# Maxima rows on ScalarE's DMA queue, normalised rows written by ScalarE, and a respaced step table in a fused attention and FFN kernel

## The reference, cut to what matters

```
x = x + L0_xattn(ln(x), ctx)     # 16 heads of 16; queries and keys normalised per head; softmax over 1601 keys
x = x + L0_ffn(ln(x))            # 256 -> 64 -> 1024, gelu, -> 64 -> 256
x = x + L1_xattn(ln(x), ctx)     # one head of 16, scores normalised per query row; the output tiled 16 times
x = x + L1_ffn(ln(x))            # soft mixture over 2048 slots; its softmax runs over the 16 batches
ln(x) = (x - mean) / sqrt(var + 1e-5)
```

## Time and profile before

| | |
|---|---|
| median of 3 runs | 6414.54 us (6410.36 to 6420.31) |
| the profiled execution | 6438.05 us, span 6436.0 us |
| TensorE matmuls busy | 5770.0 us, 90% of the span |
| TensorE weight loads busy | 2996.8 us, 47% |
| VectorE busy | 3625.0 us, 56% |
| ScalarE busy | 3263.2 us, 51% |
| GpSimd busy | 2413.9 us, 38% |
| granted TensorE clock, mean | 0.955 |
| score matmuls of stage one | from 245.1 to 4394.6 us |

### The profile page before, as it was taken

The page is one execution under the profiler, slowest core; times in us unless marked ns, Lnnn a source line. Parts: engine busy times, 40 slices in busy tenths (PEclk is TensorE's granted clock), DMA queues, the critical chain, the costliest instruction groups (busy, mean ns, idle before and its releaser), DMA issues. The chain is left out here.

```text
span 6436.0 us, 94456 instructions
## 1 busy us (share of the span) xinstructions
PE 5770.0 (90%) x36221; PEld 2996.8 (47%) x36221; DVE 3625.0 (56%) x7015; ACT 3263.2 (51%) x6257; POOL 2413.9 (38%) x2686
## 2 busy tenths in 40 slices
PE   3799999999999998999989999896599999998999
PEld 1223333333333332333323333232488888877888
DVE  3565656656666665665666656660466666652333
ACT  1366666666665666666666666663222222223331
POOL 3226356263462644626436355344122222220000
PEclk9799999999999999999999999997799999999999
DMA  2441432414324233242332432310366666666553
GB/s 57 86 86 50 78 70 63 85 51 77 70 68 83 54 77 66 70 82 60 68 67 71 79 68 65 64 23 16 135 220 214 213 215 210 208 219 243 205 196 118
DMA packets 436274, 683.75 MB, mean 106 GB/s; under 512 B 63376, under 2 KB 336928, under 8 KB 433520
## 3 DMA queue, kind: packets, MB, share of 16 engines
q1 hardware_dynamic: 326000, 568.64, 34.4%
q10 hardware_dynamic: 109824, 109.07, 5.0%
HBM read 458.39 MB, written 218.39 MB: 105 GB/s over the span
## 5 line engine op out<-in xcount | busy, mean ns | idle before, releaser
L1271 DVE TENSOR_REDUCE mx<-psum 128x1 f32<-128x401 f32 x4096 | 2166.8, 569 | 1570.2 <-PE psum L810 1565.1
L1107 ACT ACTIVATE probs<-psum 128x512 f32<-128x512 f32 (+1 forms) x3328 | 1894.1, 601 | 907.9 <-PE psum L832 900.9
L810 PE MATMUL psum<-kst,qst 96*128 96x401 bf16 x4096 | 1365.1, 348 | 86.0 <-DMA qst<-q_planes 35.9
L832 PE MATMUL psum<-qst,kst 99*128 99x512 bf16 (+1 forms) x3328 | 1302.1, 392 | 109.7 <-ACT probs L1107 58.7
L810 PEld LDWEIGHTS psum<-kst,qst 96*128 96x128 bf16 x4096 | 406.3, 99 | 1339.5 <-DVE mx L1271 900.5
L843 PE MATMUL psum<-probs,vaug 128*17 128x512 f32 x6656 | 903.0, 615 | 0.0
L1565 POOL TENSOR_TENSOR disp<-disp,rz 128x2048 f32<-128x2048 f32 x64 | 294.4, 4601 | 930.3 <-DVE rz L1795 930.3
L832 PEld LDWEIGHTS psum<-qst,kst 99*128 99x128 bf16 (+1 forms) x3328 | 335.0, 101 | 522.7 <-ACT probs L1107 262.9
L1584 PE MATMUL psum<-phi,xT 128*128 128x128 f32 x4096 | 514.3, 280 | 39.6 <-DMA xT<-xnT_scratch 33.6
L1599 PE MATMUL psum<-disp,xnb 128*128 128x128 f32 x4096 | 492.7, 279 | 52.9 <-DMA xnb<-xn_scratch 34.2
L1584 PEld LDWEIGHTS psum<-phi,xT 128*128 128x128 f32 x4096 | 482.6, 194 | 87.3 <-issue 80.9
(11 more groups left out here) (198 smaller groups left out, 7467.5 us busy)
## 6 DMA issues: line engine op xcount, KB each, us to landing
xnb<-xn_scratch SPq DMA_DIRECT2D x256, 512.0 KB, 3.7
kst<-k_planes SPq DMA_DIRECT2D x384, 200.1 KB, 8.8
logit_scratch<-disp ACTq DMA_DIRECT2D x64, 1024.0 KB, 4.9
xT<-logit_scratch SPq DMA_DIRECT2D x32, 2048.0 KB, 7.9
k_planes<-pl SPq DMA_DIRECT2D x96, 384.0 KB, 3.2
y_scratch<-ysb ACTq DMA_DIRECT2D x128, 256.0 KB, 4.9
vaug<-v_scratch SPq DMA_DIRECT2D x64, 442.0 KB, 3.7
v_scratch<-vst SPq DMA_DIRECT2D x48, 544.0 KB, 3.1
```

Source lines behind the costliest of these rows:

```text
L810: mm(to[:, 0:PW], qst[g][0:NP, j, t * P:(t + 1) * P], kst[g][0:NP, j, k0:k0 + PW], start=True, stop=True).then_inc(m_full, 1)
L832: mm(bank[S_BANK[n % 2]][0:m, :], kst[g][0:NR, j, c * P:c * P + m], qst[g][0:NR, j, :], start=True, stop=True).then_inc(s_full, 1)
L1107: fn(probs[0:m, 4 * (k % 2) + j, :], bank[S_BANK[j % 2]][0:m, :], ACT.Exp, scale=float(HD) ** 0.5).then_inc(s_exp, 1)
L1271: v.tensor_reduce(mx[:, n % 2, u // 4, u % 4:u % 4 + 1], bank[HOMES[r][0]][:, 0:PW], AX.X, ALU.max).then_inc(m_free, 1)
```

## The change

The three maxima transfers are issued by ScalarE, one after each of its first three exponentials of step 12 of a group. `lna` on GpSimd keeps only the root and makes a shift (minus mean times root) in two more small operations, and signals `ln_root`. A new item `lnx` on ScalarE writes the four tiles as `Identity` with that scale and bias. `V1` 4 to 7 get entries in `HEAD_BANK`, whose pace goes from 0.82 to 0.72. Most positions of the tail move. Bank 7 is lent out one step longer.

```diff
-    + [("kv1", 1), ("X", 1, 0), ("X", 1, 1), ("T", 3, 0), ("T", 3, 1), ("K", 8), ("K", 9), ("X", 2, 0), ("K", 10),
-       ("X", 2, 1), ("K", 11), ("kv1", 2), ("T", 4, 0), ("K", 12), ("kv1", 3), ("X", 3, 0), ("X", 3, 1), ("X", 4, 0)])
-HEAD_PACE = 0.82
+    + [("kv1", 1), ("X", 1, 0), ("X", 1, 1), ("V1", 4), ("T", 3, 0), ("V1", 5), ("T", 3, 1), ("V1", 6), ("K", 8),
+       ("V1", 7), ("K", 9), ("X", 2, 0), ("K", 10), ("X", 2, 1), ("K", 11), ("kv1", 2), ("T", 4, 0), ("K", 12), ("kv1", 3),
+       ("X", 3, 0), ("X", 3, 1), ("X", 4, 0)])
+HEAD_PACE = 0.72
...
-        put(head[done] + 0.7, 1, "ssq", n)
-        put(head[done] + 0.72, 1, "kn", n)
+        put(head[done] + 1.0, 1, "ssq", n)
+        put(head[done] + 1.02, 1, "kn", n)
...
-    put(5.67, -1, "proj", 1)
-    put(6.34, -1, "res", 1, 1)
+    put(6.0, -1, "proj", 1)
+    put(6.67, -1, "res", 1, 1)
     for t in range(QT):
-        put((5.67, 6.0, 6.67, 7.0)[t], -1, "bns", 1, t)
-        put((26.0, 26.35, 26.67, 27.0)[t], -1, "bns", 2, t)
-        put((45.67, 46.0, 46.67, 47.0)[t], -1, "bns", 3, t)
-    put(7.34, -1, "lnv", 1)
-    put(7.35, -1, "lna", 1)
-    put(7.36, -1, "base", 2)
+        put((5.67, 6.0, 7.0, 7.34)[t], -1, "bns", 1, t)
+        put((26.67, 27.0, 27.34, 27.67)[t], -1, "bns", 2, t)
+        put((45.67, 46.34, 47.0, 47.34)[t], -1, "bns", 3, t)
+    put(7.67, -1, "lnv", 1)
+    put(7.68, -1, "lna", 1)
+    put(8.34, -1, "lnx", 1)
+    put(8.35, -1, "base", 2)
...
-        put((11.34, 12.0, 12.67, 13.34, 16.67, 17.67, 18.36, 20.0)[f], -1, "V1", f)
-        put((11.67, 12.34, 13.0, 13.67, 17.0, 18.0, 19.0, 20.34)[f], -1, "gpre", f)
-        put((12.67, 13.34, 14.0, 14.67, 18.34, 19.34, 20.34, 21.34)[f], -1, "gtanh", f)
-        put((12.68, 13.35, 14.01, 14.68, 18.35, 19.35, 20.35, 21.35)[f], -1, "gpost", f)
+        if f < 4:
+            put((11.0, 11.67, 12.34, 13.0)[f], -1, "V1", f)
+        put((11.34, 12.0, 12.67, 13.34, 16.34, 17.67, 19.0, 20.67)[f], -1, "gpre", f)
+        put((12.34, 13.0, 13.67, 14.34, 17.34, 18.67, 20.0, 21.67)[f], -1, "gtanh", f)
+        put((12.35, 13.01, 13.68, 14.35, 17.35, 18.68, 20.01, 21.68)[f], -1, "gpost", f)
     for p in range(FC // 2):
-        put((16.34, 18.34, 21.67, 23.67)[p], -1, "U2", p)
+        put((15.34, 17.0, 21.0, 23.67)[p], -1, "U2", p)
...
-    put(25.34, -1, "res", 2, 0)
-    put(25.67, -1, "v2", 1)
-    put(26.34, -1, "res", 2, 1)
-    put(27.34, -1, "lnv", 2)
-    put(27.35, -1, "lna", 2)
-    put(27.36, -1, "base", 3)
-    put(29.0, -1, "xT", 2, 0)
+    put(25.67, -1, "res", 2, 0)
+    put(26.0, -1, "v2", 1)
+    put(26.67, -1, "res", 2, 1)
+    put(28.0, -1, "lnv", 2)
+    put(28.01, -1, "lna", 2)
+    put(28.67, -1, "lnx", 2)
+    put(28.68, -1, "base", 3)
+    put(29.67, -1, "xT", 2, 0)
...
-        put((36.0, 37.0, 38.34, 39.34, 40.67, 41.67, 43.0)[p], -1, "s1", p)
+        put((36.34, 37.34, 38.67, 39.67, 41.0, 42.0, 43.0)[p], -1, "s1", p)
...
-        put((44.67, 45.0, 45.67, 46.0)[t], -1, "out", t)
-        put((45.34, 45.67, 46.34, 46.67)[t], -1, "res", 3, t)
-    put(47.34, -1, "lnv", 3)
-    put(47.35, -1, "lna", 3)
+        put((44.67, 45.0, 46.0, 46.34)[t], -1, "out", t)
+        put((45.34, 46.0, 46.67, 47.0)[t], -1, "res", 3, t)
+    put(47.67, -1, "lnv", 3)
+    put(47.68, -1, "lna", 3)
+    put(48.34, -1, "lnx", 3)
...
-LENT = [s < 38 or s > 46 for s in range(STEPS)]
+LENT = [s < 38 or s > 47 for s in range(STEPS)]
...
-            def normalised(b, k):
+            def root_and_shift(b, k):
                 pool.wait_ge(ln_var, at("ln_var", b, "lnv", k))
...
                 link(pool.tensor_tensor(rs[:, :], rs[:, :], powers[:, 0:1].broadcast_to((P, QT)), ALU.pow))
-                for t in range(QT):
-                    ins = pool.tensor_scalar(xn[:, t, :], xw[:, t, :], mv[:, t, 0:1], rs[:, t:t + 1],
-                                             ALU.subtract, ALU.mult)
-                ins.then_inc(xn_ready, 1)
+                link(pool.tensor_tensor(nb[:, :], mv[:, :, 0], rs[:, :], ALU.mult))
+                pool.tensor_scalar(nb[:, :], nb[:, :], -1.0, None, ALU.mult).then_inc(ln_root, 1)
...
+            def load_maxima(n, r):
+                if r == 0:
+                    act.wait_ge(nm_ready, n + 1)
+                act.dma_start(qst[n % G][96 + r:97 + r, :, :].rearrange("o j (t q) -> o (j t) q", q=P),
+                              nT[:, r, :]).then_inc(nm_loaded, 16)
...
+            def normalised(b, k):
+                act.wait_ge(ln_root, at("ln_root", b, "lna", k))
...
+                for t in range(QT):
+                    ins = fn(xn[:, t, :], xw[:, t, :], ACT.Identity, bias=nb[:, t:t + 1], scale=rs[:, t:t + 1])
+                ins.then_inc(xn_ready, 1)
...
+                    def maximum_row(r):
+                        if c == MAX_STEP + 1 and n + 1 < B * G:
+                            load_maxima(n + 1, r)
+
                     exponentials(b, g, c, 0)
+                    maximum_row(0)
...
                     exponentials(b, g, c, 1)
+                    maximum_row(1)
...
                     exponentials(b, g, c, 2)
+                    maximum_row(2)
```

More of the change, by code:

```diff
@@ L72, in woven @@
     for label, pos in head.items():
-        put(pos, 1, *label)
+        put(pos, -1 if label[0] == "V1" else 1, *label)
     put(2.0, 1, "ln0v")
@@ L141, in woven @@
     put(1.0, -1, "kc")
-    put(31.0, -1, "cq")
-    put(31.67, -1, "cqe")
-    put(32.34, -1, "cs")
+    put(31.67, -1, "cq")
+    put(32.0, -1, "cqe")
+    put(32.67, -1, "cs")
     put(33.0, -1, "cse")
@@ L180 @@
     "pv1": ("t_mm",), "o1": ("t_act",), "out": ("t_mm",), "res": ("t_dve",), "bns": ("ln_sum",), "lnv": ("ln_var",),
-    "lna": ("xn_ready",), "base": ("based",)}
+    "lna": ("ln_root",), "lnx": ("xn_ready",), "base": ("based",)}
 def plane_buffer(b, at, label):
@@ L274, in ring_uses @@
         if home == 7:
-            b = (k - 47) // STEPS
-            if last[7] is not None and k >= 47 and (back[7] - 47) // STEPS < b:
+            b = (k - 48) // STEPS
+            if last[7] is not None and k >= 48 and (back[7] - 48) // STEPS < b:
                 homes[i] = (home, last[home], b - 1)
@@ L388, in stage_one @@
         rs = sb("rs", [P, QT])
+        nb = sb("nb", [P, QT])
         pT = sb("pT", [P, S])
@@ L444, in stage_one @@
         ln_var = sem("ln_var")
+        ln_root = sem("ln_root")
         xn_ready = sem("xn_ready")
@@ L587, in store_tail @@
                 sp.dma_start(xnT_d[b], xnT[:, :, :]).then_inc(x_stored, 16)
[L589 to L593, removed]
             steps = {"ld": load_block, "stV": store_values, "stkv1": store_keys_one, "stX": store_planes,
@@ L601, in _ @@
             alone(-1, steps)
-            load_maxima(0)
             for b in range(B):
                 for s in range(STEPS):
-                    n, c = b * G + s // KC, s % KC
-                    if c == MAX_STEP + 1 and n + 1 < B * G:
-                        load_maxima(n + 1)
                     for place in range(3):
@@ L669, in base @@
                 else:
-                    pool.wait_ge(xn_ready, at("xn_ready", b, "lna", k - 1))
+                    pool.wait_ge(xn_ready, at("xn_ready", b, "lnx", k - 1))
                 bias = (bpr, b2r, bor)[k - 1]
@@ L673, in base @@
                                    ALU.add).then_inc(based, 1)
-            def normalised(b, k):
+            def root_and_shift(b, k):
                 pool.wait_ge(ln_var, at("ln_var", b, "lnv", k))
-                if k == 1 and b >= 1:
-                    pool.wait_ge(x_stored, at("x_stored", b - 1, "st3"))
+                before = at("ln_root", b, "lna", k) - 1
+                if before >= 1:
+                    pool.wait_ge(xn_ready, before)
                 link(pool.tensor_scalar(rs[:, :], mv[:, :, 1], EPS, None, ALU.add))
                 link(pool.tensor_tensor(rs[:, :], rs[:, :], powers[:, 0:1].broadcast_to((P, QT)), ALU.pow))
-                for t in range(QT):
-                    ins = pool.tensor_scalar(xn[:, t, :], xw[:, t, :], mv[:, t, 0:1], rs[:, t:t + 1],
-                                             ALU.subtract, ALU.mult)
-                ins.then_inc(xn_ready, 1)
+                link(pool.tensor_tensor(nb[:, :], mv[:, :, 0], rs[:, :], ALU.mult))
+                pool.tensor_scalar(nb[:, :], nb[:, :], -1.0, None, ALU.mult).then_inc(ln_root, 1)
             def gelu_inside(b, f):
@@ L714, in score_inverse @@
                 pool.tensor_tensor(sg[:, :], sg[:, :], powers[:, 2:3].broadcast_to((P, QT)), ALU.pow).then_inc(sc_inv, 1)
-            steps = {"ln0a": first_norm, "kn": scaled, "X": planes, "base": base, "lna": normalised,
+            steps = {"ln0a": first_norm, "kn": scaled, "X": planes, "base": base, "lna": root_and_shift,
                      "gpre": gelu_inside, "gpost": gelu_outside, "kc": keys_centred, "sgp": score_inverse}
@@ L870, in transpose_x @@
                 if h == 0:
-                    pe.wait_ge(xn_ready, at("xn_ready", b, "lna", k))
```

(12 more changed lines are left out.)

14 lines of the change are left out of this document (7 added, 7 removed).

## The result

The changed kernel took 6546.35 us (median of 4 runs, 6539.6 to 6551.22) beside 6417.43 us for the kernel before (4 runs): a ratio of 1.0196, 95% interval 1.0171 to 1.022. The change makes the kernel 129 us slower. The prediction had 6450 us, in a range of 6350 to 6530; the measured time lies 16 us above that range. The direction was right, the size was not.

What follows compares the result with a forecast made beforehand. TensorE's own work plus stalls of its queue was taken as the bound. Gains of 3.4 and 3.0 us against losses of 7.6 and 1.5 made a batch 2.7 longer; 40 over 15 batches, less 4, gave 6450 us, range 6350 to 6530.

Steps and rivals of the forecast that it cites:

- Rows from ScalarE's queue: Maxima transfers at the fourth group and batch's end: net gain 3.4 us a batch, between -2.5 and 4.7.
- The fourth group: The fourth head group's first score waiting for maxima rows: 0.5 us left of 4.7, between 0 and 4.7.
- Steps 11 to 21: ScalarE waits for late inner GELUs: 9 us stall, 3 of clock, net loss 7.6 a batch, between 2 and 12.
- Layer two: Normalised rows written by ScalarE in step 28: stall 3.9 us, clock 2.2, net loss 1.5, between -3 and 4.
- Layer three: Normalised rows written by ScalarE around step 48: stall 2.6 us, clock 1.3, net nothing, between -2 and 2.
- Spacing: Waits for residuals and a bank wait in step 25 mostly go: gain 3.0 us a batch, between 2 and 4.
- The last tail: The final tail, running alone: 4 us saved, from three normalisations less the inner GELUs' lost overlap.
- The clock as one term: Lower-clock time, priced by place: 1.7, 1.3, 1.7 and 1.8 us removed; 3, 2.2 and 1.3 added.
- (b): Rival: stacks hold up ScalarE's queue too, the fourth group's stall stays or grows; 6515 to 6590 us, chance 0.12.
- (a): Rival: the waits go and nothing replaces them; 6310 us, or 6330 to 6390 with steps 11 to 21 unchanged; chance 0.31.

Runs made afterwards that it cites:

- e4: The changed kernel with SyncE's loads of x and the second attention's keys held until the next batch's maxima rows have landed: 6426.44 us, ratio 1.0006.
- e2: The kernel before with only the maxima rows moved to ScalarE's queue: 6537.64 us, ratio 1.0177.
- e10: The kernel before with the maxima rows on ScalarE's queue and SyncE's loads held until the rows have landed: 6441.25 us, ratio 1.0031.
- e7: The kernel before with only the last plane split, and so the stacks' loads, 0.72 of a step sooner: 6347.3 us, ratio 0.9903.
- e3: The changed kernel with the fifth to seventh tanhs and their outer halves a step or two thirds later: 6430.82 us, ratio 1.0011.
- e8: The kernel before with only the normalised rows written by ScalarE: 6365.16 us, ratio 0.9928.
- e1: The changed kernel with the maxima rows back on SyncE's queue: 6406.65 us, ratio 0.9975.
- e9: The changed kernel with rows back on SyncE, fifth to seventh tanhs later, and layer two's steps later: 6276.59 us (theory 6225 to 6270, rival 6280 to 6316).

## Why the prediction was right or wrong

**Rows from ScalarE's queue: the step that failed.** The prediction took "a landing of 1.7 to 2.3" at the end of a batch and from it "a new stall of 0.8, between 0 and 2.5", and had the part gain 3.4 us a batch. The issues came when it said. The landing was up to 5.0 us, the stall 3.3, and 9.4 us at 1.2 GHz followed, for which it had no term. Steps 51, 0 and 1 grew by 8.1 us, where the stall was bounded at 2.5. (The part of the 3.3 that comes from the later issue alone is small: with the loads held back, in e4, the stall is 0.3 us, less than the 0.8 forecast.) The 1.7 to 2.3 of the earlier trace rows were read in an order in which SyncE sends the rows first and its loads after; taking them out of that queue also takes away what held the loads back. The prediction looked at what stood ahead of the rows in SyncE's queue and not at what stood behind. e4 puts the loads back behind the rows and has 6426, within 0.4% of the 6450 that was forecast; e2 shows the part alone 113 us slower than the kernel before in its set (6424.89), and e10 takes nearly all of that back (6441).

**The fourth group: right in size, wrong in cause.** It was to keep 0.5 of its 4.7 us, and steps 38 to 40 lost 5.5. But e2 moved the queue alone and kept the stall, and e7 left the queue and lost it. The tighter packing sends the stacks off 0.72 of a step sooner, just what e7 moves alone, and the prediction had no term for it: their last issue ended 11.3 us ahead of the rows (2566.1 and 2577.4) instead of 6.6, as the timeline of the kernel after has it:

```profile
2563.31 2.77 SPq L566 DMA_DIRECT2D qst<-q_planes  x6
...
2577.38 0.53 ACTq L1109 DMA_DIRECT2D qst<-nT  x1
```

The landings over the 14 batches show the cause more closely. Counted from the end of the last stacks issue, and as means, the first of the three rows went out at 5.9 us and landed at 15.4 in the kernel before, at 8.5 and 14.6 in e7 (both on SyncE's queue), at 9.4 and 14.9 in e2 and at 8.9 and 14.4 in e10 (both on ScalarE's). The last of the stacks landed at 15.7, 14.9, 15.1 and 14.5. So on either queue the rows were in only about when the stacks ahead of them were in.

The Trainium skill (DMA: Bandwidth & Descriptors, Issuing engines are not separate DMA queues) has transfers of all engines interleave on the same 16 DMA engines. The trace agrees at both places: rows from ScalarE took 5.3 us behind the stacks in e10, and up to 5.0 beside loads in the kernel after, against 1.7 alone. The turn-taking that the prediction set against it (the Trainium skill, same page, Queues, rings and completion order) did not let them pass at the speed of an idle queue: behind the stacks they took 3.4 us in e2's batch and 5.3 in e10's.

**Steps 11 to 21: right mechanism, sizes off both ways.** The fifth inner GELU was to end 43.0 us after step 11 began; it did so at 43.6 (2434.68 to 2478.3). The forecast was 71 us for the stretch; it was 68.2 in that batch and 68.6 in the mean. The stall was 6.2 us where 9 were taken, within 5 to 13, and the clock more than the 3 us of loss taken: 15.1 us at 1.2 GHz against 2.7. e3 removes most of both by moving tanhs 4 to 6 and their outer halves alone, and gains 8.2 us a batch, of which 3.8 are idle time. The other 4.4 are the price of 11.7 us fewer at 1.2 GHz, 0.38 for each. The net loss of 7.6 came out as 5.1 of length. At that price, 3.1 us more idle and 12.4 more at 1.2 GHz come to about 7.8, an estimate; products that moved to other stretches account for the rest.

**Layer two: the chain as forecast, the net loss smaller.** The root was to be ready 6.4 us into step 28 and was at 6.0; four writes were to take 1.9 and took 2.07; the stall was to be 3.9 and was 4.0 (11.50 with 7.53 busy). Of the loss of 1.5 us there is less: steps 26 to 30 idle 0.9 us more but spend 1.0 less at 1.2 GHz, and are 2.1 shorter, in part because products moved across the stretch's ends. e8 adds that the writing by ScalarE is a gain when the plane split does not come first. **Layer three** was to stall TensorE for 2.6 us at the writes; steps 47 to 50 idle 2.1 us, of which 0.9 stands behind the writes (an exponential in step 48), and their clock stays full: 1.1 us gained where the forecast was 0. **Spacing** was to gain 3.0: in the stretches without a stall of their own (2 to 10, 22 to 25, 31 to 37, 41 to 46) the idle time fell from 8.6 to 5.1, so 3.5. **The last tail** was to save 4 us; from the last score to the span's end it was 2041.4 before (4394.6 to 6436.0) and 2042.8 after (4497.7 to 6540.5): nothing.

**The clock as one term.** Over the parts, the prediction took away 1.7, 1.3, 1.7 and 1.8 us of clock and put in 3, 2.2 and 1.3: no change. Measured, a batch has 14.4 us more at 1.2 GHz; at the 0.38 us for each that e3 gives that is an estimated 5.5 of the 6.4 us by which a batch grew. Most of it stands behind the stalls of step 51 (3.3 us, none before) and of step 17 (4.5, where the kernel before had 1.8 in step 16 and 0.7 in step 17).

**The rivals.** (b) named 6515 to 6590 and the time was 6546. Its premise, that the stacks hold ScalarE's queue up too, is what e10 shows (5.3 us, over the 4 that was to decide it), but the time was not lost that way: its stall was to stay at the fourth group, which lost it. The contention that cost the time came at the batch's end, from loads that the change itself set free, so that (b)'s number came out in part by luck. (a) came true only in the experiments, at 6277 to 6316, when the two bad parts are mended.

**What stays open.** The same kind of stall is not always followed by the lower clock: the 4.0 us of idle in steps 28 and 29 had a clock of 1.00 in the batch shown, 3.2 us at 1.2 GHz in the mean of the kernel after, none in e1 and 4.9 in e3 and e4. Nor does it take a long stall: the clock fell in step 32 of all 14 batches of e9 behind a single wait of 0.9 us, in step 14 of all 14 of the kernel after behind one of 1.5 to 1.7, and in step 16 of 11 of the kernel before behind waits of 0.6 and 1.15. Why it falls at one wait and not at another was not settled. It is why e9 fell between its two theories: the 5.1 us at 1.2 GHz in steps 31 to 37 are those behind the 0.9.

## What to carry to other kernels

When a transfer leaves a queue, look at what stood behind it as well as ahead: the next loads start sooner and run beside it, and its old latency no longer holds. A wait that put the bulk behind it restored the old length of a batch here (e10). Price a stall with the spell at the lower clock behind it, which behind the unbroken stalls of 3 to 5 us in steps 17 and 51 cost as much again or more; shorter waits were followed by such a spell too, in some places and not in others. When a stall disappears with a change of many parts, move each part alone before giving it the credit: here the stall went because the loads went out sooner, and the part that was meant for it cost 113 us.

## What the runs showed of the hardware

- A transfer issue on ScalarE runs beside its ACTIVATE: in the kernel after, issues of 0.58, 0.57 and 0.58 us at 2635.81, 2636.45 and 2637.09 stood beside exponentials of 0.59 us that began 0.63 us apart.
- The three maxima rows (one partition each) landed after 1.7 us with the DMA engines 0.05 busy (e10, 2854.93 to 2858.33), after up to 5.0 beside SyncE's loads of x, keys and stacks (the kernel after), and after 5.3 (e10) or 5.1 (e7) when issued 8 to 9 us behind the stacks, from ScalarE's or from SyncE's queue.
- After an idle stretch of 3.4 us at a batch's end TensorE ran some 10 us at 1.2 GHz, though it then had work without a break (13.09 busy of 13.09 at a clock of 0.62); the mean of 14 batches is 3.3 us idle and 9.4 at 1.2 GHz in steps 0 and 1.
- Four ACTIVATEs of 128x256 with scale and bias per partition take 2.07 us back to back (586 ns each by their records); the four GpSimd writes that they replace took 4.85.
